# Float32r parts for the projections and score products of three cross attention layers

## The reference

```
q = norm(x) @ Wq + bq ; k = ctx @ Wk + bk ; v = ctx @ Wv + bv      (per head: 128 x 16 and 12544 x 16)
s = q @ k.T / sqrt(16) + mask                                       (128 x 12544 per head)
x = x + softmax(s) @ v   (in layers 1, 2 and 3 through one more matrix, Wo)
```

## Time and profile before

| | |
|---|---|
| median of three runs | 2795.91 us |
| the profiled execution | 2791.38 us |
| its span | 2789.6 us |
| mean granted TensorE clock | 0.938 |
| L0x, first to last instruction in the span | 3.88 to 577.3 us |
| L2x | 1460.1 to 2031.4 us |

### The profile page before, as it was taken

One profiled execution on the slowest core, in us unless ns is written; L12 is line 12 of the kernel. 1 busy time (PEld: TensorE's weight loads), 2 busy tenths in 40 slices (PEclk: granted clock), 3 DMA queues, 4 the chain that ended last, 5 costly groups with the idle time before them and its releaser, 6 DMA issues. The chain is left out here.

```text
span 2789.6 us, 76444 instructions
## 1 busy us (share of the span) xinstructions
PE 2545.4 (91%) x31295; PEld 1895.6 (68%) x31295; DVE 1540.3 (55%) x3557; ACT 1460.4 (52%) x2953; POOL 293.6 (11%) x415
## 2 busy tenths in 40 slices
PE   7999999978999999995679999999947999999958
PEld 4777777766777777774535777777734777777738
DVE  3455545525888888886534544555433455554532
ACT  2555555534777777771133555555512555555521
POOL 2110111002112222200001000000002101111000
PEclk9999999989999999996579999999958999999969
DMA  3222222155444443421043222222113122222116
GB/s 86 46 53 56 57 57 43 16 171 151 115 113 101 105 107 104 109 64 40 1 140 85 55 42 55 49 48 42 15 43 89 43 56 57 57 46 54 17 49 217
DMA packets 114955, 198.78 MB, mean 71 GB/s; under 512 B 20515, under 2 KB 56884, under 8 KB 114685
## 3 DMA queue, kind: packets, MB, share of 16 engines
q1 hardware_dynamic: 114686, 194.86, 28.6%
HBM read 115.65 MB, written 0.13 MB: 42 GB/s over the span
## 5 line engine op out<-in xcount | busy, mean ns | idle before, releaser
L1065 DVE TENSOR_REDUCE L3x_tops<-L3x_m_bank 128x1 f32<-128x448 f32 x448 | 262.7, 620 | 266.0 <-PE L3x_m_bank L871 265.8
L1065 DVE TENSOR_REDUCE L0x_tops<-L0x_m_bank 128x1 f32<-128x448 f32 x448 | 262.8, 620 | 263.6 <-PE L0x_m_bank L871 263.3
L1065 DVE TENSOR_REDUCE L2x_tops<-L2x_m_bank 128x1 f32<-128x448 f32 x448 | 262.8, 620 | 258.7 <-PE L2x_m_bank L871 258.3
L454 ACT ACTIVATE L1x_prob<-L1x_p_s,L1x_neg_max 128x512 f32<-128x512 f32 (+1 forms) x400 | 276.0, 690 | 115.8 <-DVE L1x_neg_max L565 113.1
L997 ACT ACTIVATE L3x_prob<-L3x_s_bank 128x512 f32<-128x512 f32 x448 | 219.7, 543 | 168.6 <-PE L3x_s_bank L883 168.6
L997 ACT ACTIVATE L0x_prob<-L0x_s_bank 128x512 f32<-128x512 f32 x448 | 219.7, 543 | 166.9 <-PE L0x_s_bank L883 166.9
L997 ACT ACTIVATE L2x_prob<-L2x_s_bank 128x512 f32<-128x512 f32 x448 | 219.7, 543 | 166.6 <-PE L2x_s_bank L883 166.6
L560 DVE CUSTOM_DVE_ANT_0 L1x_p_s<-L1x_p_s,L1x_mask 128x512 f32<-128x512 f32 (+1 forms) x400 | 273.7, 684 | 39.0 <-PE L1x_p_s L320 32.0
L329 PE MATMUL L1x_p_t<-net_ident,L1x_prob 128*128 128x128 f32 x1568 | 239.9, 274 | 10.1 <-ACT L1x_probT L175 9.9
L871 PE MATMUL L3x_m_bank<-L3x_k_stack,L3x_q_max 32*128 32x448 f32 x896 | 237.5, 596 | 6.0 <-DMA L3x_k_stack<-L3x_kT 3.2
L871 PE MATMUL L0x_m_bank<-L0x_k_stack,L0x_q_max 32*128 32x448 f32 x896 | 235.4, 591 | 6.4 <-DMA L0x_k_stack<-L0x_kT 3.6
(11 more groups left out here) (678 smaller groups left out, 4247.2 us busy)
## 6 DMA issues: line engine op xcount, KB each, us to landing
L1x_k_stack<-L1x_kT SPq DMA_DIRECT2D x288, 128.0 KB, 2.4
L3f_w<-in_L_ffn_w SPq DMA_DIRECT2D x16, 1024.0 KB
L0x_ctx<-in_ctxT SPq DMA_DIRECT2D x14, 896.0 KB, 4.7
L0x_k_stack<-L0x_kT SPq DMA_DIRECT2D x112, 112.0 KB
L2x_ctx<-in_ctxT SPq DMA_DIRECT2D x14, 896.0 KB
L2x_k_stack<-L2x_kT SPq DMA_DIRECT2D x112, 112.0 KB, 4.3
L3x_ctx<-in_ctxT SPq DMA_DIRECT2D x14, 896.0 KB, 4.8
L3x_k_stack<-L3x_kT SPq DMA_DIRECT2D x112, 112.0 KB
```

Of the source, the lines that this page charges most:

```text
L454: e.activation(prob[:, h % P_RING, 0:nk], p_s[h % S_RING][:, 0:nk], ACT.Exp, bias=neg_max[:, odd, h:h + 1]).then_inc(sem("exped"), 1)
L1065: e.tensor_reduce(tops[:, b % 2, 4 * j + r, half:half + 1], m_bank[n % RING][:, 0:HALF], AX, ALU.max).then_inc(sem("m_free"), 1)
```

## The change

In layers 0, 2 and 3, each float32 operand of the key and value projections and of both score products is split into a high part, rounded to float32r, and a low part, the rest rounded again. A product becomes three: high x high, high x low, low x high.

- Projections: the weights and the context are held in two parts. Each item is three products of the two chunks, accumulated, six float32r matmuls in place of two float32 products. GpSimd splits the context of each block (two passes over 128 x 1792), with one context buffer in place of two. ScalarE writes the high part of the keys, and VectorE writes the low part (`k_low`, four times per block). A new projection of keys waits for `k_split`.
- Scores and maxima: the three products of a head are stacked over the contraction rows. A head takes 48 rows, two rows for the maximum's two parts and two for the mask's, in a group of 64 rows. Two heads of a wave lie side by side in the two groups. `k_stack` has eight slots instead of four. The score products are done in one float32r pass. The maxima and scores of one step now use the same two groups.
- Stacking: 24 DMAs per block in place of eight, each again of 16 rows by 2 slots by 3584 bytes, in order of the quads, with one semaphore per quad. The mask rows come after them, four DMAs per block of eight slots each, read from a copy in device memory that is made once per layer.
- Order: LAG is 9 in place of 7, the rise of the accumulator's scale is two steps later, and the transpose of the queries is two transposes and their copy has 256 columns.
- The maximum is kept in `top` and split into two columns of `nat` (two small VectorE instructions per quad).

```diff
-SLOTS4 = 4
+QUADS = 4
+SLOTS = 8
-LAG = 7
+LAG = 9
+GROUP = 64
+MROWS = 112
+TOP, MASK = 3 * HD, 3 * HD + 2
+PRODUCTS = ((HIGH, HIGH), (HIGH, LOW), (LOW, HIGH))
...
             def load(b):
                 if b >= 2:
-                    e.wait_ge(sem("projected"), (b - 1) * ITEMS)
-                e.dma_start(ctx[:, b % 2], ctx_dram[:, :, b * KB2:(b + 1) * KB2]).then_inc(sem(f"ctx_loaded_{b % 2}"), 16)
+                    e.wait_ge(sem("ctx_split"), b - 1)
+                elif b:
+                    e.wait_ge(sem("ctx_0_split"), 1)
+                    e.wait_ge(sem("ctx_0_high"), 1)
+                e.dma_start(ctx[:], ctx_dram[:, :, b * KB2:(b + 1) * KB2]).then_inc(sem("ctx_loaded"), 16)
+
+            def stack(b):
+                odd = b % 2
+                e.wait_ge(sem("k_split"), b * 4 + 4)
+                for j in range(QUADS):
+                    if b >= 2:
+                        e.wait_ge(sem("s_made"), s_done(s_at((b - 2) * WAVES + 4 * j + 3, 1)))
+                    for r in range(2):
+                        for n, (_, part) in enumerate(PRODUCTS):
+                            at, of = GROUP * r + HD * n, HD * (2 * j + r)
+                            e.dma_start(k_stack[at:at + HD, odd, j::4, :].bitcast(F32),
+                                        kT[of:of + HD, part].bitcast(F32)).then_inc(sem(f"k_stacked_{odd}_{j}"), 16)
                 if mask_kind:
...
+                    for r in range(2):
+                        for part in (HIGH, LOW):
+                            at = GROUP * r + MASK + part
+                            e.dma_start(k_stack[at:at + 1, odd].bitcast(F32),
+                                        mask_dram[part:part + 1].bitcast(F32)[:, b * KB2:(b + 1) * KB2].unsqueeze(1).broadcast_to([1, SLOTS, KB2])
+                                        ).then_inc(sem(f"mask_stacked_{odd}"), 16)
...
+            def split_ctx(b):
+                odd = b % 2
+                e.wait_ge(sem("ctx_loaded"), (b + 1) * 16)
                 if b >= 2:
+                    e.wait_ge(sem("projected"), (b - 1) * ITEMS)
+                e.tensor_copy(ctx_part[:, odd, HIGH], ctx[:]).then_inc(sem("ctx_high"), 1)
+                e.wait_ge(sem("ctx_high"), b)
+                e.tensor_tensor(ctx_part[:, odd, LOW], ctx[:], ctx_part[:, odd, HIGH].bitcast(F32),
+                                ALU.subtract).then_inc(sem("ctx_split"), 1)
...
-                    for c in range(DC):
-                        mm = e.matmul(bank[:, 0:HALF], wk[:, c, part * P:(part + 1) * P],
-                                      ctx[:, odd, c, half * HALF:(half + 1) * HALF], start=c == 0, stop=c == DC - 1)
+                    for (wp, cp), c, start, stop in steps:
+                        mm = e.matmul(bank[:, 0:HALF], wk_part[:, wp, c, part * P:(part + 1) * P],
+                                      ctx_part[:, odd, cp, c, half * HALF:(half + 1) * HALF], start=start, stop=stop)
...
-                if g % WAVES == 0 and i == 0:
-                    e.wait_ge(sem(f"k_stacked_{b % 2}"), (b // 2 + 1) * (12 if mask_kind else 8) * 16)
+                if g % 4 == 0 and r == 0:
+                    e.wait_ge(sem(f"k_stacked_{b % 2}_{j}"), (b // 2 + 1) * 6 * 16)
+                    if mask_kind and j == 0:
+                        e.wait_ge(sem(f"mask_stacked_{b % 2}"), (b // 2 + 1) * 64)
...
                     if i == 0 and b:
-                        e.wait_ge(sem(f"k_stacked_{(b - 1) % 2}"), ((b - 1) // 2 + 1) * (12 if mask_kind else 8) * 16)
-                    e.activation(kT[:, part, half * HALF:(half + 1) * HALF], bank[:, 0:HALF], ACT.Identity,
-                                 bias=bias_k[:, part:part + 1]).then_inc(sem("evacuated"), 1)
+                        for j in range(QUADS):
+                            e.wait_ge(sem(f"k_stacked_{(b - 1) % 2}_{j}"), ((b - 1) // 2 + 1) * 6 * 16)
+                    e.activation(kT[:, HIGH, part, half * HALF:(half + 1) * HALF], bank[:, 0:HALF], ACT.Identity,
+                                 bias=bias_k[:, part:part + 1]).then_inc(sem("k_high"), 1)
...
+            def k_low(b, i, bank):
+                part, keys = i // 2, slice(i % 2 * HALF, (i % 2 + 1) * HALF)
+                e.wait_ge(sem("k_high"), 4 * b + i + 1)
+                e.scalar_tensor_tensor(kT[:, LOW, part, keys], bank[:, 0:HALF], bias_k[:, part:part + 1],
+                                       kT[:, HIGH, part, keys].bitcast(F32), ALU.add, ALU.subtract).then_inc(sem("k_split"), 1)
...
+                if g % 2 == 1 and g // WAVES + 1 < NB and g % WAVES < 8:
+                    k_low(g // WAVES + 1, g % WAVES // 2, p_proj)
```

More of the change, by code:

```diff
@@ L650, in cross_attention_turned @@
     has_wo = "wo" in w
+    rows_used = MASK + 2 if mask_kind else MASK
     xn = sb("xn", [P, D])
@@ L878, in scores @@
                 e.wait_ge(sem("s_free"), s_done(s_at(u, 1) - RING))
-                for t in tiles_of(half):
-                    for i, r in enumerate(heads_of(u)):
-                        rows = slice(32 * r, 32 * r + 32)
-                        at = t - tiles_of(half)[0]
-                        mm = e.matmul(s_bank[s_at(u, i) % RING][:, at * P:(at + 1) * P],
-                                      k_stack[rows, b % 2, j, t * P:(t + 1) * P], q_sub[rows, j, :], start=True, stop=True)
+                for at, t in enumerate(tiles_of(half)):
+                    for r in range(2):
+                        mm = e.matmul(s_bank[s_at(u, r) % RING][:, at * P:(at + 1) * P],
+                                      k_stack[rows_of(r), b % 2, slot_of(u), t * P:(t + 1) * P],
+                                      q_sub[rows_of(r), slot_of(u), :], start=True, stop=True)
                         if t == tiles_of(half)[-1]:
@@ L889, in turn_q @@
                 n = s_q_at(q)
-                e.wait_ge(sem("raised"), q + 1)
+                e.wait_ge(sem("raised"), 3 * q + 3)
                 if n >= S_GROUP:
                     e.wait_ge(sem("s_free"), s_done(n - RING))
-                e.transpose(s_bank[n % RING][:, 0:P], nat[:, q // 4 % 3, q % 4, :], ident[:]).then_inc(sem("s_made"), 1)
+                for p in range(2):
+                    mm = e.transpose(s_bank[n % RING][:, p * P:(p + 1) * P], nat[:, 4 * p + q % 4, :], ident[:])
+                mm.then_inc(sem("s_made"), 1)
             def values(k):
@@ L902, in values @@
                 e.wait_ge(sem("s_free"), s_done(s_at(2 * k + 1, 1)))
-                for t in tiles_of(half):
-                    for r in range(4):
-                        mm = e.matmul(p_oT[32 * r:32 * r + VW, j * P:(j + 1) * P], v[:, b % 2, t, 4 * j + r, :],
-                                      prob[:, k % 3, r, t - tiles_of(half)[0], :], start=t == 0, stop=t == NT - 1)
+                for at, t in enumerate(tiles_of(half)):
+                    for n in range(4):
+                        mm = e.matmul(p_oT[32 * n:32 * n + VW, j * P:(j + 1) * P], v[:, b % 2, t, n // 2 * 8 + 2 * j + n % 2, :],
+                                      prob[:, k % 3, n, at, :], start=t == 0, stop=t == NT - 1)
                 mm.then_inc(sem("valued"), 1)
@@ L924, in _ @@
             mm.then_inc(sem("xn_turned"), 1)
+            e.wait_ge(sem("k_weights_split"), 1)
+            e.wait_ge(sem("ctx_0_split"), 1)
+            for i, bank in enumerate([p_proj] + m_bank):
+                project(0, i, bank)
             e.wait_ge(sem("q_weights"), 32)
@@ L934, in _ @@
             project(0, 6, s_bank[0])
-            e.wait_ge(sem("evacuated"), 1)
+            e.wait_ge(sem("k_split"), 1)
             project(0, 7, p_proj)
-            e.wait_ge(sem("nat_filled"), 1)
+            e.wait_ge(sem("nat_filled"), 3)
             e.wait_ge(sem("nat_set"), 2)
-            for j in range(SLOTS4):
-                mm = e.transpose(s_bank[1][:, j * P:(j + 1) * P], nat[:, 0, j, :], ident[:])
+            for s in range(SLOTS):
+                if s == 4:
+                    e.wait_ge(sem("k_split"), 4)
+                bank = s_bank[1] if s < 4 else m_bank[0]
+                mm = e.transpose(bank[:, s % 4 * P:(s % 4 + 1) * P], nat[:, s, :], ident[:])
             mm.then_inc(sem("q_turned"), 1)
-            e.wait_ge(sem("q_max_made"), 1)
-            e.wait_ge(sem("evacuated"), ITEMS)
+            e.wait_ge(sem("q_max_made"), 2)
+            e.wait_ge(sem("minus_stacked"), 128)
+            e.wait_ge(sem("v_made"), 4)
             for g in range(LAST_G):
@@ new lines, in _ @@
+            e.wait_ge(sem("v_weights_high"), 1)
+            e.tensor_tensor(wv_part[:, LOW], wv[:], wv_part[:, HIGH].bitcast(F32), ALU.subtract).then_inc(sem("v_weights_split"), 1)
+            e.wait_ge(sem("k_bias"), 16)
+            for i, bank in enumerate([p_proj] + m_bank):
+                k_low(0, i, bank)
+            e.wait_ge(sem("q_made"), 1)
+            e.wait_ge(sem("nat_set"), 2)
+            heads = nat[:].rearrange("q s (r e) -> q (s r) e", r=2)
+            made = s_bank[1][:, 0:D].rearrange("q (h d) -> q h d", h=HX)
```

277 lines of the change are left out of this document (148 added, 129 removed).

## The result

The changed kernel takes 3222.36 us (median of four runs, 3215.5 to 3226.07) against 2795.35 us for the kernel before: ratio 1.152, 95% interval 1.148 to 1.155, so 427 us slower. I had forecast 2934 and a range to 3080: the direction was right, the size was not. The profiled execution has a span of 3213.7 us and a mean granted clock of 0.830.

What follows compares the result with a forecast made beforehand. TensorE alone bounds these layers before, the stacking's waits after. Layer changes of +70 (L0x), +3 (L2x) and +70 (L3x) sum to +143 on 2791, giving 2934 us; own range 2850 to 3010, 8-in-10 range 2770 to 3080.

Steps and rivals of the forecast that it cites:

- the cycle of L0x and L3x: In masked blocks the first maxima wait for masks, last in the queue: 43.5 us per block against 37.93.
- TensorE's own block: TensorE's work per block: 30.7 us against 37.9, with key items at 1.33 and waves at 0.76 or 0.65.
- The stacking: Per block, 24 key DMAs at 0.82 us each land 22.3 us after the first issue, the masks at 23.0.
- The clock after the wait: Half speed on TensorE after a block's wait for the masks: 2.3 us charged, bounds 0 and 3.2.
- Edits that cost nothing: GpSimd's split of the context, about 6 us per block, lies in some 25 us of idle time.
- The idle time: TensorE idles some 10 us per masked block: wave 16 13.7 us after wave 8, masks landing about 24.5 after it.
- rival 2: The stacking is hidden: blocks of 30.7 + 1.6 us, total 2600; chance 0.05.
- The end of a layer: Last block and end of L0x: VectorE's reductions 20.5, nine waves of scores 10.4, the end 6.9; 38 us.
- The start: In L0x the masks for the first maxima land 40.3 us after the layer's start.
- L2x: ScalarE's evacuation waits for all 24 DMAs, `kT` being one buffer: block 38.5 us, layer 574.1 against 571.3.
- 1 (the issue's pace): Stacking goes at the issue's 0.65 us per DMA: blocks of 39.5 and 33.5, total 2765; chance 0.12.
- Rival 3's second half: A stacking DMA costs 1.05 us: total about 3090; chance 0.16, shared with two cases of dearer float32r products.

Runs made afterwards that it cites:

- Experiments 1 to 3: Edits of the changed kernel: mask DMAs after the first six key DMAs (3008.72 us), two `kT` buffers with masks last (3149.45 us), both (2687.03 us).
- experiment 3: Changed kernel with mask DMAs issued after the first six key DMAs and `kT` in two buffers: 2687.03 us.
- experiment 7: Changed kernel with each quad's six key DMAs issued product by product, alternating row groups: 3098.77 us.
- experiment 8: Changed kernel with 45 unread products on TensorE before a block's first maxima in L0x and L3x: 3112.89 us.
- experiment 6: Changed kernel with GpSimd's split of the context waiting for the second quad's maximum: 3171.94 us.
- experiment 4: Changed kernel with only 8 key DMAs per block from the third block on, output not the reference's: 2841.95 us (one run).
- experiment 5: Changed kernel with 8 key DMAs per block from the third block on, plus GpSimd's context split waiting for the second quad's maximum: 2737.65 us.
- experiment 9: Changed kernel with 6 unread products after each of waves 1, 3, 5 and 7 in the last block of L0x, L2x and L3x: 3213.11 us.

## Why the prediction was right and wrong

The main mechanism was forecast right, its prices were not, and one cost was put at nothing (GpSimd's split). What failed are two steps of the sum: the cycle of L0x and L3x, put at 43.5 us and measured at 50.5, and their last block, put at 38 us and measured at 65.8 (69.3 in L3x). By term:

- **What bounds the kernel: right.** TensorE gets cheaper, the stacking becomes the limit. Experiments 1 to 3 take away its two waits and with them 535 of the 3222 us.
- **TensorE's own block: too low, 34.5 against 30.7 + 1.6 for `k_low`'s stalls.** The key item (1.41 for 1.33) and the wave (0.79 and 0.68 for 0.76 and 0.65) account for 0.8, one wait of scores for ScalarE per block for 0.9; 0.5 is left open. The stalls were right, 1.6 (experiment 3). No row isolates the 0.1 us charged per wave for changing the grouping of the array; from a wave's first maxima to its first scores it takes 0.30 us (368.09 to 368.39), where 0.22 + 0.1 were charged. The stretch from the first maxima to the stacking was right: 15.1 + 1.6 + 1.5 = 18.2 against 18.4 in experiment 3.
- **The stacking: mis-sized.** From the first key DMA to the first maxima I had 23.0 us; it takes 25.8 to 27.5. The keys' last landing is at 23.4 to 24.4 (22.3): 0.855 us per DMA for 0.82. That three in a row read the same rows I had named as an upper bound and not priced; by experiment 7 their order is what costs, through the rows read or those written. The masks follow 2 to 3 us behind, not 0.7: their own four issues take 2.7. Cost: 3.4 us per block.
- **The clock after the wait: mis-sized.** 8.6 us at 1.2 GHz cost 4.3 us of full-speed work; I charged 2.3. That is the block shown. Over the thirteen blocks of L0x the time from the first maxima to the next stacking is 23.8 us in the mean, 18.4 of work and 1.5 of collision, which leaves about 4 for the clock: some 3 us in the shorter blocks and 6 in the longer ones. Experiment 8 gives 3.2 of it back. In the earlier trace rows the half-clock stretch was 6 us, and I charged less than half of it.
- **"Edits that cost nothing": wrong for GpSimd's split.** I looked for idle time on GpSimd to hold it and not for what runs beside it. It costs 1.5 us of TensorE's time per block, 1.3 by experiment 6, and where the block is short a dip of the clock as well (104 us in 39 blocks, 2.7 each, between experiments 4 and 5).
- **These make the cycle.** 43.5 + 3.4 + 1.5 + 2.0 = 50.4 us; measured 50.5 from stacking to stacking and 50.2 from first maxima to first maxima.
- **The idle time: right by luck.** I had "some 10 us", from 24.5 to the masks' landing less 13.7 from wave 8 to wave 16, and 10.0 was measured. The 13.7 are wrong: my own prices give 15.5 (8 x 0.71 + 4 x 0.90 + 5.7 + 0.54), and TensorE needs 18.0 (322.43 to 340.43). The longer stacking made up for it. The cycle doesn't use this number; rival 2 was put aside with it.
- **The end of a layer: wrong.** 38 us for the last block and the drain; 65.8 measured. 20 us are the clock (experiment 8), the rest is that the block at full clock takes 45 to 48. I priced that stretch from VectorE's reductions and full-clock waves, and never asked at which clock a block without projections would run.
- **The start: 5 us short**, 45.4 us for 40.3 from the layer's start to the first maxima, of which 3.9 are the longer stacking.
- **L2x: the mechanism right, the cycle 41.0 for 38.5.** The 2.5 are the last landing (23.3 for 22.3) and the collision (1.5; experiment 6 takes 1.1 off the period). That this adds up is in part luck: the low clock, 6.5 us per block in the mean, costs 3.3 and not the 2 that I charged, so something else on that path is 1.3 shorter than priced, and what it is stays open. The cycles are some 35 of the 47 us missed in L2x; its last block with the end took 51.6 us for 42.5, the last 19 us of it at half clock.

For L0x the terms add up: 45.4 + 13 x 50.2 + 65.8 = 763.8, against 40.3 + 13 x 43.5 + 38 = 643.8. Of the 120 us missed, 87 are the cycle, 28 the end and 5 the start.

Of the rivals, 1 (the issue's pace) was wrong for this order of DMAs; in the other order the issue comes near it (0.70 us), but the landings don't and the total is 3099, not 2765. Rival 3's second half was the nearest in kind, a dearer DMA, though at 0.855 and not 1.05; its 3090 lacks the clock and the collision. Rival 2 had 2600 for a hidden stacking. Hidden it gives 2687 (experiment 3); 2617 took three more edits, one of them against the stalls that rival 2 had counted in, so the two numbers meet by luck.

The gain on TensorE is 37.93 - 33.3 = 4.6 us per block. How much of it would come from the projections alone, which need no more DMAs, was not run.

## What to carry to other kernels

When a faster engine hands the limit to a queue of transfers, look at the order in the queue and at the buffer they read before counting bytes: here the waits for the same 28 DMAs cost 535 us, and a second buffer and four DMAs moved forward took them away. An edit counted as hidden must be checked twice, for time on its own engine and for what it blocks on others while it runs. And each wait on TensorE is to be priced with the clock behind it, up to the end of the layer if the work behind it is thin.

## What the hardware showed unasked

- The last block of L0x ran at a granted clock of 0.50 (1.2 GHz) for 65.8 us although TensorE was busy for 59.42 of them. With 24 products of 448 columns added it stood at 1.00 from 9.3 us after the first maxima and for 26 us on (experiment 9), and begun at full clock the unchanged work had 0.91 in the mean (experiment 8).
- After a gap of 1.5 us on TensorE the clock fell in 22 of 30 blocks, for 3 to 10 us (experiment 4); without the gap it stayed at 1.00 from the first maxima to the next stacking (experiment 5).
- VectorE's 128x4 cast in SBUF stands still while GpSimd casts 128x1792: 1.63 us for 0.16. The Trainium skill ("SBUF — State Buffer", "SBUF: two separate sides") has it that GpSimd and VectorE, where VectorE runs in a mode that uses two ports, share one pair of ports, and that the instruction which starts first holds it to its end. The trace agrees, though it doesn't show the mode: GpSimd's cast starts 0.08 us before VectorE's and ends 0.03 us before it.
- 24 DMAs of 112 KB between the same two buffers land 0.84 us apart if three in a row read the same 16 rows and write into one half of the partitions, and 0.75 apart if both alternate (issue 20.5 and 16.8 us). In the kernel before, with three in a row that read the same rows and write the same partitions, they land 1.04 us apart.
